# Relative attention scores: query heads written four times over, contraction over 32 rows instead of 8

## The reference, cut to what matters

```
q = hidden @ Wq.T + bq            # also k, v
qh = q.reshape(B, T, H, D).transpose(0, 2, 1, 3)   # also kh, vh
score1 = einsum('bhqd,bhkd->bhqk', qh, kh)
rel_k  = rel_k_emb[clip(q_pos - k_pos, -128, 128) + 128]      # (T, T, D)
s2     = einsum('bhqd,qkd->qbhk', qh, rel_k)      # for each query position q its own 8 x 128 matrix
attn   = softmax((score1 + s2) / sqrt(8))
out    = attn @ vh + (the same with rel_v_emb)     # then out @ Wo.T + bo, added to the residual
```

## Time and profile before

| | us |
|---|---|
| median of 3 runs | 1342.63 (1341.35 to 1342.88) |
| the profiled execution | 1347.9 |
| its span, first to last instruction | 1344.4 |
| mean granted TensorE clock, share of full speed | 0.912 |

### The profile page before, as it was taken

One profiled execution on the slowest core, in us unless ns is written; L12 is line 12 of the kernel. 1 busy time (PEld: TensorE's weight loads), 2 busy tenths in 40 slices (PEclk: granted clock), 3 DMA queues, 4 the chain that ended last, 5 costly groups with the idle time before them and its releaser, 6 DMA issues. The chain is left out here.

```text
span 1344.4 us, 22573 instructions
## 1 busy us (share of the span) xinstructions
PE 1191.2 (89%) x8762; PEld 828.9 (62%) x8766; DVE 685.3 (51%) x2125; ACT 513.7 (38%) x1165; POOL 432.8 (32%) x512
## 2 busy tenths in 40 slices
PE   6999988999978875898789799989899999978896
PEld 5877766788833243466467556755567774565575
DVE  5545543344559635576467356638722136745212
ACT  5534232443345532345344442414343323432231
POOL 7959530000045423673467240011000010041404
PEclk9999988999975577899899988999989988988998
DMA  5000231422066000000000000000101000002202
GB/s 167 1 4 1 85 119 47 127 64 64 1 212 156 1 1 32 1 1 1 0 1 1 1 10 1 1 1 2 72 31 48 32 15 1 1 4 90 87 21 47
DMA packets 51625, 52.24 MB, mean 39 GB/s; under 512 B 19552, under 2 KB 42336, under 8 KB 50496
## 3 DMA queue, kind: packets, MB, share of 16 engines
q1 hardware_dynamic: 50496, 48.71, 11.6%
q0 software_dynamic: 1024, 2.10, 0.7%
HBM read 43.59 MB, written 7.21 MB: 38 GB/s over the span
## 5 line engine op out<-in xcount | busy, mean ns | idle before, releaser
L636 ACT ACTIVATE scratch<-bank 128x512 f32<-128x512 f32 x96 | 52.4, 594 | 77.2 <-PE bank L535 77.2
L451 POOL TENSOR_TENSOR ln_rstd<-ln_ve,ln_half 128x4 f32<-128x4 f32 x28 | 28.7, 1025 | 156.0 <-DVE ln_ve L430 155.9
L595 DVE TENSOR_REDUCE scratch<-bank 128x4 f32<-128x512 f32 x96 | 61.6, 683 | 21.6 <-PE bank L519 13.1
L2783 POOL TENSOR_TENSOR scratch<-scratch 128x16 f32<-128x16 f32 x16 | 51.7, 3231 | 50.0 <-DVE scratch L3125 50.0
L1137 ACT ACTIVATE scratch<-bank 128x512 f32<-128x512 f32 x64 | 38.2, 597 | 67.9 <-PE bank L1096 67.9
L1106 PEld LDWEIGHTS bank<-scratch 128*128 128x128 f32 x512 | 59.5, 192 | 7.2 <-issue 7.2
L1156 DVE SCALAR_TENSOR_TENSOR x_res<-bank,scratch,x_res 128x128 f32<-128x128 f32 x64 | 18.0, 344 | 88.1 <-PE bank L1106 88.1
L601 DVE TENSOR_TENSOR scratch<-bank,scratch 128x512 f32<-128x512 f32 x96 | 61.4, 681 | 0.0
L1096 PE MATMUL bank<-xnT,scratch 128*128 128x512 f32 x128 | 60.1, 616 | 0.0
L1106 PE MATMUL bank<-scratch 128*128 128x128 f32 x512 | 59.6, 275 | 0.0
L535 PE MATMUL bank<-ident,scratch 128*128 128x128 f32 x384 | 53.3, 282 | 3.6 <-DVE scratch L601 3.6
(11 more groups left out here) (582 smaller groups left out, 2936.3 us busy)
## 6 DMA issues: line engine op xcount, KB each, us to landing
scratch<-conv_kernels SPq DMA_DIRECT2D x8, 1024.0 KB, 11.1
scratch<-e_l_ffn_w SPq DMA_DIRECT2D x20, 256.0 KB, 3.0
scratch<-e_l_ffn_w SPq DMA_DIRECT2D x4, 1024.0 KB, 15.1
values<-scratch SPq DMA_DIRECT2D x8, 512.0 KB, 2.8
scratch<-values SPq DMA_DIRECT2D x8, 512.0 KB, 4.4
weights<-w_l_ffn SPq DMA_DIRECT2D x1, 3698.0 KB, 12.5
scratch<-e_l_ffn_w SPq DMA_DIRECT2D x4, 768.0 KB, 9.1
weights<-w_l_attn SPq DMA_DIRECT2D x1, 2560.5 KB, 9.2
```

The costliest lines, as they stand in the source:

```text
L595: self.nc.vector.tensor_reduce(self.top[:, n % 4, :], self.by_head(self.core.ps[n % 4][:, :]), AX_X, ALU.max, negate=True).then_inc(self.t ...
L636: self.nc.scalar.activation(self.prob_of(n), self.by_head(self.core.ps[4 + n % 2][:, :]), ACT.Exp, scale=scale) \
L2783: nc.gpsimd.tensor_tensor(rn, ss, power, ALU.pow).then_inc(rooted.sem, rooted.up())
```

## The change

Query weights are laid out a second time, each head's 8 columns four times over (16 heads times 32 columns, 512 columns, 256 KB), at the end of the block's weights. They land in the part of the weight buffer that is used as `outs` later in the block. The query-head products then have 32 columns and fill all 32 PSUM rows of each group, with the same 8 features four times. The bias is laid out to match. The rounds contract over 32 rows, which sums the same product four times, and the evictions multiply by one quarter. The two unused products ahead of each of rounds 2 to 7 are taken out.

```diff
+    outs = w.take(B * 16, 8)
+    wq_copies = outs.rearrange("p n d -> p (n d)")[:, 0:16 * 32].rearrange("p (h c) -> p h c", h=16)
...
-    ROUNDS, PART = 8, 4
+    ROUNDS, PART, COPIES = 8, 4, 4
...
-                        m = nc.tensor.matmul(ps[HEAD_BANKS[n]][32 * g:32 * g + 8, u * 2 * P:(u + 1) * 2 * P]
-                                             .rearrange("p (b m) -> p b m", b=B), wq[:, 8 * h:8 * h + 8],
+                        m = nc.tensor.matmul(ps[HEAD_BANKS[n]][32 * g:32 * g + 32, u * 2 * P:(u + 1) * 2 * P]
+                                             .rearrange("p (b m) -> p b m", b=B),
+                                             wq_copies[:, h, :],
...
                     pe.wait_ge(rel_out_act.sem, rel_out_act.at(2 * r - 3))
-                    core.keep_clock_bf(4 * (r % 2), 2)
                     pe.wait_ge(rel_out_dve.sem, rel_out_dve.at(2 * r - 3))
...
-                        q, rows = query_of(r, t, g), slice(32 * g, 32 * g + 8)
+                        q, rows = query_of(r, t, g), slice(32 * g, 32 * g + 32)
...
-                    nc.scalar.copy(*made_in(r, g)).then_inc(rel_out_act.sem, rel_out_act.up())
+                    nc.scalar.mul(*made_in(r, g), 1.0 / COPIES).then_inc(rel_out_act.sem, rel_out_act.up())
...
-                    nc.vector.tensor_copy(*made_in(r, g)).then_inc(rel_out_dve.sem, rel_out_dve.up())
+                    nc.vector.tensor_scalar(*made_in(r, g), 1.0 / COPIES, None, ALU.mult).then_inc(rel_out_dve.sem, rel_out_dve.up())
...
-    placed = np.tile(np.pad(g[n + "bq"].reshape(16, 8).T, ((0, 24), (0, 0))), (4, 1))
+    placed = np.tile(g[n + "bq"].reshape(16, 8).T, (16, 1))
...
+                          np.tile(g[n + "Wq"].T.reshape(D, 16, 1, 8), (1, 1, 4, 1)).reshape(D, 512))
```

More of the change, by code:

```diff
@@ L2424, in layer_l2_attn @@
     bq1, bv, bo, relk, relv = w.take(1), w.take(D), w.take(D), w.take(2 * P), w.take(P, 8)
+    outs = w.take(B * 16, 8)
+    wq_copies = outs.rearrange("p n d -> p (n d)")[:, 0:16 * 32].rearrange("p (h c) -> p h c", h=16)
     heads_of = w.take(32, 16 * B).rearrange("p m (h b) -> p m h b", h=16)
-    sm = RelativeHeads(core, c, wo, more=Carve(core.xnT), o=w.take(B * 16, 8))
+    sm = RelativeHeads(core, c, wo, more=Carve(core.xnT), o=outs)
     relative_out = heads_of.rearrange("p m h b -> p (m h b)").rearrange("p (b h d) -> p b h d", b=B, h=16)
@@ L3838, in lay_weights @@
                           np.tile(g[n + "rel_k_emb"][255::-1].T, (16, 1)),
-                          g[n + "rel_v_emb"][at])
+                          g[n + "rel_v_emb"][at],
+                          np.tile(g[n + "Wq"].T.reshape(D, 16, 1, 8), (1, 1, 4, 1)).reshape(D, 512))
     def two_heads(a):
```

## The result

| | before | after |
|---|---|---|
| median of the first four runs, us | 1341.99 (1340.96 to 1342.88) | 1329.91 (1326.35 to 1332.32) |
| ratio of the runs | | 0.9903, 95% interval 0.9883 to 0.9922 |
| ratio in two later measurements of the same kernel | | 0.993 (0.991 to 0.995); 0.9908 (0.9875 to 0.9942) |
| profiled execution | 1347.9, span 1344.4 | 1326.35, span 1324.5 |

The forecast was 1332.1 us, a saving of 10.5 of 1342.63, which is a ratio of 0.9922. The direction and the place were right, the size was short by 2.5 us. The miss is a narrow one: the two medians of the table differ by 12.1 us, which would lie inside the range, and the interval's upper end is the forecast ratio itself.

What follows compares the result with a forecast made beforehand. It took TensorE alone, at half clock with unused products on the path, to set the rounds' 2.99 us period. Savings 10.5 + 0.1 - 0.1 = 10.5 us from 1342.63 gave 1332.1 us, range 1329.8 to 1337.6.

Steps and rivals of the forecast that it cites:

- The clock stays at 1.00 with 32 rows: In the rounds, products using all 128 rows keep full clock: about 0.95 us a round instead of 2.02.
- Rival 2: In the rounds the clock falls and comes back as TensorE waits for VectorE: 2.8 us less saved, 1335; chance 0.07.
- rivals 3 and 4: Query heads' column groups stop running side by side, 1352.5 us, chance 0.04; VectorE's factor evictions take whole gain, chance 0.01.
- rival 1: Clock ignores rows and stays at half through the rounds; only removed unused products save, 5.4 us, 1337.3; chance 0.12.
- VectorE sets the rounds, 1.33 us each: In the rounds VectorE becomes the bound: two evictions take 1.29 us, the loop 1.32 each, taken as 1.33.
- the loop: Rounds through both buffers: 1.24 to VectorE's first copy, 1.29 copies, 0.11 until TensorE starts; 2.64 us for two rounds.
- Evictions with a factor at the copy's price: In the rounds, VectorE's eviction with an immediate factor costs the copy's 686 ns; other end 752, 0.8 us more.
- heads at the old price: Query heads with 32 columns keep about 7.1 us; 0.1 us added, 2.8 as the far end.
- weights hidden: The block's weight DMA grows from 1035 to 1291 KB but is issued a block ahead; uncovered it would cost 1.4 us.
- Transposes 10.4 to 10.7 us earlier, and 0.1 shorter: Behind the rounds, transposes start between 803.3 and 803.6 instead of 813.99, and gain 0.1 us from full clock.
- Outside the block nothing changes but the place of later stages against the clock's steps: Outside the changed block, only later stages' place against clock steps shifts; 1.5 us allowed either way.

Runs made afterwards that it cites:

- e5: Changed kernel with rounds contracting over 16 of the 32 rows of each group, factor one half: 1334.86 us, ratio 0.9935 to the kernel before.
- e2: Kernel before with only the two unused products ahead of rounds 2 to 7 taken out, still 8 rows: 1334.02 us, ratio 0.9938.
- e3: Changed kernel with the two unused products put back ahead of rounds 2 to 7: 1331.84 us, ratio 0.9927 to the kernel before.
- e4: Kernel before with only the 512 weight columns added to the load, not used: 1341.55 us, ratio 0.9992.

## Why the prediction was wrong, step by step

- **The clock stays at 1.00 with 32 rows.** Right (in all six executions with 32 rows), and by e5 the rows are the cause. Rival 2, a clock that falls because TensorE now waits, did not come: TensorE was busy 7.04 of 7.80 us. Nor did rivals 3 and 4. The Trainium skill's account of the gate by busyness alone (TensorE: Matmul & The Clock Gate, "What's actually happening"; rival 1) doesn't hold here: in e2 and e5 TensorE was busy all the time and had 0.50.
- **VectorE sets the rounds, 1.33 us each.** Right: 1.34. Its second source, the loop, is what binds, and takes 2.68 us for two rounds where I had 2.64. The difference is a reading: the earlier trace rows has the first product at 791.34, so the step from VectorE to TensorE is 0.15 and not 0.11. One term beside it was off without harm: in the loop a round's products took 1.10 us at full clock (e3), where I took 0.95 from rounds 0 and 1, which still take 2.07 for both. What makes the later ones longer was not tested.
- **Evictions with a factor at the copy's price, heads at the old price, weights hidden.** All right: 684 ns, 7.1 us in all, and 0.9992 in e4.
- **Transposes 10.4 to 10.7 us earlier, and 0.1 shorter.** Right: from the first eviction to the transposes it was 813.99 - 792.58 = 21.41 us and is 798.10 - 787.20 = 10.90, so 10.5 earlier, and 10.6 at the first reduction.
- **Rival 1's price** of 5.4 us was short. Without fillers the rounds at half clock follow in 1.80 us and not 2.02, so it would have been 6.5 (e2). I had taken the 2.02 us to the first filler's load as the round's, and only the fillers' 0.97 as saved, where each round came 1.19 sooner.
- **"Outside the block nothing changes but the place of later stages against the clock's steps; I allow 1.5 us either way."** This is the step that failed, as a size. The stretch from 391 to 510 us took from 113.2 to 118.3 us in ten executions, all with the same instructions, and the stretch behind the block 219.7 to 223.5. Single executions of the changed kernel ranged from 1326.35 to 1341.4. The first ratio's interval is 0.2% either way, 2.6 us, and I had seen three runs of before that agreed within 1.5 us, and took their agreement for the spread, although the profiled execution lay 5.3 us above their median. The prediction itself said that a measurement tells no less than 2.7 us, and the low end of my range was 2.3 us under the forecast. All three intervals hold a saving of 10.6 us, so the block's gain alone is compatible with each, and that the first ratio fell outside the range can be chance.

Whether the whole excess of the first measurement, 2.5 us over the forecast, is chance stays open; a part may be the change's after all. The four executions whose rounds ran at half clock (before, e2, e4, e5) took 223.4 us from the block's end to the 1125.6 mark, each to 0.02. The six with 32 rows took 219.7, 220.4, 220.9, 223.1, 223.1 and 223.5, on average 221.8, 1.6 less. In the trace's record of the granted clock, the last fall in the block lies 6.0 to 6.1 us before its last VectorE instruction in all four half-clock kernels, and 5.6 to 8.2 us before it in the six. This would fit a slow stretch that ends on a clock step and so sets all that follows to the same place against the steps, and its absence that leaves the place to chance. That was not tested: no run forces the place while leaving the block as it is. Nor is the place enough: in the changed kernel's own three executions that last fall lies 5.7, 5.6 and 5.8 us before the block's end, and the stretch behind took 219.7, 223.1 and 223.5. With 1.6 us more the expected saving would be about 12 us, by an estimate from these single executions, and the three ratios give 13.0, 9.4 and 12.4. Against it stands the stretch from 510 to 773, which takes 262.8 us in before and e4, with 34.1 us of it at half clock, and 264.8 in all others, with 37.5: if that were the change's, it would take 2 us back. Why it does so stays open too.

## What to carry to other kernels

Products that leave rows of their row groups unused can hold TensorE at half clock though it is never idle, as 8 and 16 of 32 rows did here, and where operands can be replicated at their source for nothing, filling the rows is better than unused products, which cost time of their own (11.53 us for the stretch against 13.18 with both). Price such a step by the loop that binds next, here the evictions through two PSUM halves, which capped the gain. Two parts of a change that overlap have no shares of their own: the fillers are worth 6.5 us alone and 1.65 on top of the rows. In a kernel with many clock steps, take the spread from enough runs before setting a range: the block was foretold to 0.1 us, the whole only to 2.5.

## What the runs showed of the hardware

- With 8 or 16 rows in each of four row groups, TensorE ran without a gap (10.74 of 10.74 us in e2, 7.0 of 7.0 in e5) at a granted clock of 0.50; with 32 rows it held 1.00 at 90% busy (7.04 of 7.80 us, after). Products of 128 rows and 8 columns held 1.00 for 7 us too.
- These float32 products took the same time whatever their rows: rounds 0 and 1 together 2.07 us at 1.00 with 8, 16 and 32 rows (before, e5, after), a later round 1.80 us at 0.50 with 8 and 16 (e2, e5). The query heads took 7.1 us in all with 8 and with 32 columns.
- On VectorE a multiplication by an immediate, PSUM to SBUF, 128x512, took 684 ns, like the copy; the one addition of an operand in SBUF took 752.
